# State-space stage: steps handled in two halves, row stores dealt out over the steps, the skip term as a product on TensorE

## The reference, cut to what matters

```
xn    = rms_norm(resid) * norm_w
skip  = xn @ skip_w.T ;  x = silu(conv4(xn @ in_w.T) + conv_b)
delta = softplus(x @ wd1.T @ wd2.T + wd2_b) ;  B = x @ wB.T ;  C = x @ wC.T
h[e,n] = exp(delta[e] * A[e,n]) * h[e,n] + delta[e] * x[e] * B[n]      # over time
y[e]   = sum_n h[e,n] * C[n] + W_D[e] * x[e]
out    = resid + (y * silu(skip)) @ out_w.T
```

## Time and profile before

| | us |
|---|---|
| median of 3 runs | 2874.22 (2873.86 to 2876.11) |
| profiled execution, its own time | 2880.12 |
| its span, first to last instruction | 2878.4 |
| first piece of `mamba` on TensorE | at 813.5 |
| first scan (L1114) | at 969.9 |
| last step's product (L1122) | starts at 2044.3 |
| experts' first TensorE work | at 2074.6 |

### The profile page before, as it was taken

The page is one execution under the profiler, slowest core; times in us unless marked ns, Lnnn a source line. Parts: engine busy times, 40 slices in busy tenths (PEclk is TensorE's granted clock), DMA queues, the critical chain, the costliest instruction groups (busy, mean ns, idle before and its releaser), DMA issues. The chain is left out here.

```text
span 2878.4 us, 33375 instructions
## 1 busy us (share of the span) xinstructions
PE 2290.2 (80%) x10578; PEld 1579.3 (55%) x10578; DVE 1978.3 (69%) x2641; ACT 1324.5 (46%) x2201; POOL 1167.5 (41%) x579
## 2 busy tenths in 40 slices
PE   1789999988713578888888887978599999999960
PEld 0677777776500223333323332323299999999960
DVE  6564555565400478888898988899588888888844
ACT  1333222233112555555556555643277666676630
POOL 1120221222055969787887878795100000000026
PEclk7899999999855689998989899978799999999985
DMA  6011100111042001111010111010265555555545
GB/s 229 15 37 36 36 5 31 36 36 36 26 165 83 21 31 37 37 37 37 37 52 29 46 37 37 30 51 22 73 235 212 212 215 220 222 222 221 220 128 187
DMA packets 109900, 264.86 MB, mean 92 GB/s; under 512 B 15796, under 2 KB 88516, under 8 KB 95124
## 3 DMA queue, kind: packets, MB, share of 16 engines
q1 hardware_dynamic: 103700, 247.41, 23.9%
q0 software_dynamic: 6144, 16.79, 1.8%
HBM read 213.89 MB, written 50.27 MB: 92 GB/s over the span
## 5 line engine op out<-in xcount | busy, mean ns | idle before, releaser
L946 POOL TENSOR_TENSOR m_work<-m_ux,m_bb 128x2048 f32<-128x2048 f32 x128 | 578.4, 4525 | 197.1 <-DVE m_hh L1114 196.4
L1187 PE MATMUL m_y<-m_work,m_ident 128*128 128x512 f32 x1024 | 553.8, 691 | 0.8 <-DVE m_work L1122 0.8
L1058 ACT ACTIVATE m_da<-m_dl,m_A 128x512 f32<-128x512 f32 x512 | 347.9, 687 | 304.5 <-DVE m_hh L1114 304.3
L1114 DVE TENSOR_TENSOR_SCAN m_hh<-m_da,m_work 128x512 f32<-128x512 f32 x256 | 295.7, 1207 | 230.4 <-POOL m_work L946 157.7
L1187 PEld LDWEIGHTS m_y<-m_work,m_ident 128*128 128x128 f32 x1024 | 213.9, 220 | 346.6 <-issue 345.0
L1602 PE MATMUL e_h<-e_xTh,e_w1h 128*128 128x256 f32 x1248 | 356.0, 285 | 16.8 <-DVE e_xTl L1538 16.8
L1671 POOL DMA_INDIRECT c_ya<-scratch_yg,c_dst x64 | 66.1, 1033 | 732.8 <-DMA c_wts<-scratch_wts 713.6
L1602 PE MATMUL e_h<-e_xTh,e_w1l 128*128 128x256 f32 x1248 | 351.7, 282 | 0.0
L1602 PE MATMUL e_h<-e_xTl,e_w1h 128*128 128x256 f32 x1248 | 351.6, 282 | 0.0
L1114 DVE TENSOR_TENSOR_SCAN m_hh<-m_da,m_carry,m_work 128x512 f32<-128x512 f32 x256 | 310.4, 1267 | 58.4 <-ACT m_da L1058 45.3
L1122 DVE TENSOR_TENSOR m_work<-m_hh,m_cb 128x2048 f32<-128x2048 f32 x128 | 292.8, 2288 | 11.4 <-issue 0.4
(11 more groups left out here) (238 smaller groups left out, 4664.0 us busy)
## 6 DMA issues: line engine op xcount, KB each, us to landing
e_w<-in_w SPq DMA_DIRECT2D x39, 2048.0 KB, 7.5
e_w<-in_w SPq DMA_DIRECT2D x39, 1024.0 KB, 9.5
m_bb<-scratch_bT SPq DMA_DIRECT2D x32, 1024.0 KB, 4.6
e_xg<-scratch_xg SPq DMA_DIRECT2D x39, 256.0 KB, 9.6
scratch_yg<-e_yo SPq DMA_DIRECT2D x39, 256.0 KB, 9.7
scratch_xg<-x1p SPq DMA_DIRECT2D x19, 512.0 KB, 7.8
e_b<-in_b SPq DMA_DIRECT2D x39, 128.0 KB, 8.7
xt<-in_x SPq DMA_DIRECT2D x9, 512.0 KB, 5.7
```

The source lines that it names most:

```text
L946: pool.tensor_tensor(bx[:, g % NB], ux[q % 2][:], slot.to_broadcast([P, KE, T]), ALU.mult).then_inc(s_bx, 1)
L1058: act.activation(da[e % 2][:], dl[q % 2][:, e], ACT.Exp, scale=A[:, at:at + 1]).then_inc(s_exp, 1)
L1114: dve.tensor_tensor_scan(hh[:, e], da[e % 2][:], bx[:, g % NB, e], 0.0 if q % 2 == 0 else carry[:, n, e:e + 1], ALU.mult, ALU.add).then_in ...
L1187: last = mm(y[:, e], ident[:], hc[:, g % 2, e], start=(n == 0), stop=(n == NST - 1))
```

## The change

1. **Half steps.** VectorE handles blocks 0 and 1 (two scans, then their product with C's row), then blocks 2 and 3. The product has half the length and there are two of them. The waits on `s_hc` and `s_carry` count halves. ScalarE's `extra` is cut in two: a half behind `decay(g, 3)` and a half behind `decay(g + 1, 1)`; the copy for `carry` is cut in two as well.
2. **A new table of slots.** One piece per step, issued between the sums of the first half and those of the second (`MID`). The input projections move to n = 10 and 12 to 14 of the chunk before the last one, O1 from n = 5 to n = 9, and ScalarE's copies with them (O1's is at n = 10, second half).
3. **Row stores dealt out.** GpSimd issues one of the 64 indirect stores every second step; SyncE loads the rows a block of 128 at a time into a buffer of their own.
4. **Skip term.** Four 128x128 diagonal matrices of `W_D` are made once by ScalarE. At n = 0, TensorE starts `y` with `diag * x`; L1099 is gone.
5. **C's broadcast.** `spread(g + 1)` is issued when the second half's product is done, ahead of the second half's sums (behind the first half's and the piece); at n = 0 it is ahead of all four sums, behind the piece, the wait for `finish` and the skip products.
6. **Softplus.** GpSimd's `(z + 1) - 1` (L919) becomes two ScalarE instructions; one of GpSimd's sums moves from n = 11 to n = 12. ScalarE's relu is written to `dl` directly. `conv` of block 0 moves to n = 15 of the chunk before, the others to n = 0 to 2.
7. The output rows are stored in two halves.

```diff
-    ahead = {0: ["IN2"], 1: ["IN3"], 2: ["SK0", "SK1"], 3: ["SK2", "SK3"], 4: ["O0"], 5: ["O1"], 6: ["BD"], 7: ["DT0", "DT1"],
-             8: ["DT2", "DT3"], 14: ["IN0"], 15: ["IN1"]}
+    TOP, MID = 0, 1
+    ahead = {(n, MID): [g] for n, g in enumerate(("SK0", "SK1", "SK2", "SK3", "O0", "BD", "DT0", "DT1", "DT3", "O1",
+                                                  "IN0"))}
+    ahead |= {(12 + e, MID): [f"IN{e + 1}"] for e in range(KE - 1)}
+    TAKEN = [(11, 1), (13, 0), (14, 0), (15, 0)]
+    ahead[8, TOP] = ["DT2"]
...
         @block.gpsimd
...
+                if n == NST - 1 and q + 2 < NCH:
+                    conv(q + 2, 0)
...
+                if n < KE - 1:
+                    conv(p, n + 1)
+                if n == 11:
+                    pool.wait_ge(s_wm, 2 * p + 2)
+                    pool.tensor_tensor(w, ez, w, ALU.subtract).then_inc(s_c, 1)
+                if n == 12:
+                    pool.wait_ge(s_c, p + 1)
                     pool.wait_ge(s_ln, p + 1)
                     pool.tensor_tensor(lw, lw, w, ALU.add).then_inc(s_lw, 1)
                     pool.wait_ge(s_lw, p + 1)
+                    pool.tensor_tensor(dl[p % 2][:], lw, dl[p % 2][:], ALU.add).then_inc(s_dl, 1)
...
             for g in range(STEPS):
                 if g + 2 < STEPS:
                     inputs(g + 2)
+                if g % 2 == 0:
+                    spread_rows(g // 2)
                 extra(g // NST, g % NST)
...
         @block.scalar
...
+            for e in range(KE):
+                act.activation(diag[:, e], ident[:], ACT.Copy, scale=column("W_D", e)).then_inc(s_diag, 1)
...
+            def extra(q, n, half):
+                p, p2 = q + 1, q + 2
+                if 0 <= p2 < NCH:
+                    if (n, half) in TAKEN:
+                        take_in(p2, TAKEN.index((n, half)))
+                    if n >= 14:
+                        taps(p2, n - 14, half)
                 if 0 <= p < NCH:
                     if n < 2:
+                        taps(p, n + 2, half)
+                    if 1 <= n < 5 and half == 0:
+                        take_skip(p, n - 1)
+                    if n == 4 and half == 1:
                         silu(p)
+                    if n == 6 and half == 0:
                         take_rows(p)
                     if n in (7, 8):
+                        take_step(p, 2 * (n - 7) + half)
                     if n == 9:
+                        wait_drained(act, f"DT{2 * half + 1}", p)
+                        both = ez[:, HALF * half:HALF * (half + 1)]
+                        act.activation(both, both, ACT.Exp, scale=-1.0).then_inc(s_ez, 1)
                     if n == 10:
+                        act.wait_ge(s_ez, 2 * p + 2)
+                        if half == 1:
+                            act.wait_ge(s_wm, 2 * p + 1)
+                        act.activation(w, ez if half == 0 else w, ACT.Identity, bias=1.0 - 2.0 * half).then_inc(s_wm, 1)
+                    if n == 11 and half == 0:
                         act.activation(lw, ez, ACT.Ln, bias=1.0).then_inc(s_ln, 1)
+                if q > 0 and (n, half) in ((5, 0), (10, 1)):
+                    take_out(q - 1, half)
...
                 decay(g, 2)
+                keep(g, 0)
                 decay(g, 3)
+                extra(q, n, 0)
                 if g + 1 < STEPS:
                     decay(g + 1, 0)
+                keep(g, 1)
                 if g + 1 < STEPS:
                     decay(g + 1, 1)
+                extra(q, n, 1)
...
         @block.vector
...
-                for e in range(KE):
-                    dve.scalar_tensor_tensor(out=y[:, e], in0=xs[p % 2][:, e], scalar=column("W_D", e), in1=y[:, e],
-                                             op0=ALU.mult, op1=ALU.add).then_inc(s_yf, 1)
-                dve.wait_ge(s_yf, (p + 1) * KE)
...
+                for j in range(2):
+                    cols = slice(HALF * j, HALF * (j + 1))
...
+                    for e in range(cols.start, cols.stop):
+                        dve.wait_ge(s_exp, g * KE + e + 1)
+                        dve.tensor_tensor_scan(hh[:, e], da[e % 2][:], bx[:, g % NB, e],
+                                               0.0 if q % 2 == 0 else carry[:, n, e:e + 1], ALU.mult, ALU.add).then_inc(s_scan, 1)
+                    if n == 0 and j == 1 and q > 0:
+                        finish(q - 1)
+                    dve.wait_ge(s_cb, g + 1)
...
+                    dve.tensor_tensor(hc[:, g % 2, cols], hh[:, cols],
+                                      cb[:].rearrange("p (o t) -> p o t", o=1).to_broadcast([P, HALF, T]), ALU.mult).then_inc(s_hc, 1)
...
         @block.tensor
...
+                pieces(q, n, TOP)
+                if n == 0:
+                    pieces(q, n, MID)
+                    if q > 0:
+                        pe.wait_ge(s_y1, q)
+                    pe.wait_ge(s_silu, 2 * q + 1)
+                    for e in range(KE):
+                        mm(y[:, e], diag[:, e], xs[q % 2][:, e], start=True, stop=False)
+                    pe.wait_ge(s_hc, 2 * g + 2)
                     spread(g + 1)
+                for j in range(2):
+                    pe.wait_ge(s_hc, 2 * g + j + 1)
+                    if j == 1 and n > 0 and g + 1 < STEPS:
+                        spread(g + 1)
+                    for e in (HALF * j, HALF * j + 1):
+                        last = mm(y[:, e], ident[:], hc[:, g % 2, e], start=False, stop=(n == NST - 1))
+                    if j == 0 and n > 0:
+                        pieces(q, n, MID)
```

More of the change, by code:

```diff
@@ L798, in mamba @@
         ux = [sb(f"ux{h}", [P, KE, T]) for h in range(2)]
-        brow = [sb(f"brow{h}", [2 * NST, T]) for h in range(2)]
-        dr = sb("dr", [DR, T])
+        drb = sb("drb", [DR + 2 * NST, T])
+        dr = drb[0:DR]
+        brow = [drb[DR:DR + 2 * NST], sb("brow1", [2 * NST, T])[:]]
+        diag = sb("diag", [P, KE, P])
         bb = sb("bb", [P, 2, NG, T])
@@ L803, in mamba @@
         bx, hc = work[:, 0:NB], work[:, NB:NB + 2]
[L804 removed]
+        rows = sb("rows", [P, 2, D])
         hh = sb("hh", [P, KE, T])
[L806 removed]
+        mo = sb("mo", [P, 2, D])
         dst = sb("dst", [P, NPICK], I32)
@@ L962, in _ @@
                     inputs(g + 2)
+                if g % 2 == 0:
+                    spread_rows(g // 2)
                 extra(g // NST, g % NST)
+            for i in range(2):
+                pool.wait_ge(picks_out[i], 16 * NPICK // 2)
         @block.scalar
@@ L972, in take_in, with taps @@
                 act.activation(region(p, e), rb[:], ACT.Copy).then_inc(drained, 1)
-            def taps(p, e):
+            def taps(p, e, half):
                 wait_drained(act, f"IN{e}", p)
@@ L980, in taps @@
                 at = (p % 2) * T
-                for k in range(PAD):
+                for k in (0, 1) if half == 0 else (2,):
                     act.activation(pk[:, e % 2, k], xpad[:, e, at + k:at + k + T], ACT.Copy, scale=conv_w(e, k)).then_inc(s_pk, 1)
-                act.activation(pk[:, e % 2, PAD], region(p, e), ACT.Identity, scale=conv_w(e, PAD),
-                               bias=column("conv_b", e)).then_inc(s_pk, 1)
+                if half == 1:
+                    act.activation(pk[:, e % 2, PAD], region(p, e), ACT.Identity, scale=conv_w(e, PAD),
+                                   bias=column("conv_b", e)).then_inc(s_pk, 1)
             def take_skip(p, e):
@@ L1012, in take_out @@
                 wait_filled(act, f"O{j}", p)
-                if p >= 1:
-                    act.wait_ge(mo_out, 16 * p)
-                act.activation(mo[:, 2 * j:2 * j + 2], rb[:].rearrange("p (s d) -> p s d", s=2), ACT.Copy).then_inc(drained, 1)
-            def extra(q, n):
-                p = q + 1
-                if n >= 14 and 0 <= q + 2 < NCH:
-                    take_in(q + 2, n - 14)
-                    if n == 15:
-                        taps(q + 2, 0)
+                if 2 * p + j >= 1:
+                    act.wait_ge(mo_out, 16 * (2 * p + j))
@@ L1058, in decay, with keep @@
                 act.activation(da[e % 2][:], dl[q % 2][:, e], ACT.Exp, scale=A[:, at:at + 1]).then_inc(s_exp, 1)
+            def keep(g, j):
+                q, n = g // NST, g % NST
+                if q % 2 == 0:
+                    act.wait_ge(s_scan, g * KE + HALF * (j + 1))
+                    if q >= 2:
+                        act.wait_ge(s_scan, ((q - 1) * NST + n + 1) * KE)
+                    cols = slice(HALF * j, HALF * (j + 1))
+                    act.activation(carry[:, n, cols], hh[:, cols, T - 1], ACT.Copy).then_inc(s_carry, 1)
             act.wait_ge(s_pad, 1)
-            extra(-2, 14)
-            extra(-2, 15)
-            for n in range(NST):
-                extra(-1, n)
+            for q, n in slots[:6 + NST]:
+                for half in range(2):
+                    extra(q, n, half)
             decay(0, 0)
@@ L1150, in piece @@
                     wait_drained(pe, "BD", p)
```

(24 more changed lines are left out.)

163 lines of the change are left out of this document (69 added, 94 removed).

## The result

The changed kernel takes 2749.4 us (median of 4 runs, 2746.4 to 2761.7), the kernel before 2874.0 (4 runs, 2873.7 to 2876.1). The ratio is 0.957, 95% interval [0.954, 0.960]: 124.6 us less. The run of 2761.7 had a mean granted clock of 0.88, the three others 0.92 to 0.93. The profiled execution took 2748.59 us and its span is 2746.8, 131.6 shorter than the span of before. The other 7 us are that before's profiled execution lay 6.1 over the median of these runs and this one 0.8 under its own.

A forecast was written before the change was run, and what follows sets the result against it. VectorE was taken to set the steps' pace, behind a chain at the head. -63.4 - 4.5 - 2 - 121 + 81 = -110, from 2880.1 to 2770, less 5.9: 2764 us; range 2708 to 2815, its own 2740 to 2790.

The forecast's parts named there:

- Head: Before the first scan: stores gone from ahead of the first convolution, L919 on ScalarE, one convolution moved ahead; -63.4 us.
- Tail: After the last product: the last four L1099 instructions go and only half of the sums is left; -4.5 us.
- VectorE's own work: VectorE in the steps: half products and paired scans cost +17 us, the L1099 groups removed save 19; net -2.
- The old waits: VectorE's waits in the steps for ScalarE's decay and GpSimd's inputs, plus small gaps for C's row: removed whole, -121 us.
- the new waits: VectorE's waits in the half steps, counted from zero over the eight chunks: 81 us in sum.
- IN0 behind O1: Input projection at n = 10 waits for the output piece's late copy, delaying C's row: 2.5 us a chunk.
- The boundary: Between chunks: skip products delay the broadcast (1.2 us), GpSimd's late convolutions delay decays (0.6 and 2.7): 4.5 us.
- The clock as a term of its own: TensorE's broadcast at the lower clock level after idling: 1.4 us a chunk, 12 us in chunks 1 to 5.
- Row stores: GpSimd's stores in the steps: 8 a chunk, 10.2 us, hidden except at chunk boundaries; bounds of one 0.97 and 3.0.
- B: Steps: most new waits don't come, 30 us instead of 81, giving 2713 us; chance 0.2.
- C: TensorE's queue: sums and piece ahead of C's broadcast at low clock cost 43 us more, giving 2804; chance 0.24.
- D: TensorE becomes the bound of the steps, with granted clock under 0.74; slower, for instance 2895 us; chance 0.04.

The follow-up runs named there:

- the second trace of the change: The changed kernel run again unchanged on the chip of the follow-up runs: 2752.4 us (5 runs), ratio 0.9579 to the kernel before.

## Why the forecast was right, and where its steps were off

The forecast was 2764 us (2708 to 2815), the result 2749.4, inside the likeliest case's own range (2740 to 2790). Between the two profiled executions the difference is larger: -110 forecast, -131.6 measured. It came from steps that were mis-sized; from the medians it is only 15, as before's profiled execution lay 6.1 us over its kernel's median and the new one 0.8 under.

**Head**, -63.4 forecast, -65.3 measured. The chain was read rightly: the table load is at 849.08 (850.7 forecast) and the first scan at 904.55 (906). The first convolution, at 826.35, came 1.8 us before its forecast, mostly because the stage's first loads had landed 1.4 us earlier (TensorE's first piece starts at 812.14, before at 813.50).

**Tail**, -4.5 forecast, -8.1 measured. The four instructions and half of the sums went as said. What was missed is the output piece: 3.69 us after an idle of 2.48 here, where the tail of before had 6.37 after 5.24. With the skip term back on VectorE it was 5.50 after 5.24. The last 0.8 us are an earlier start of the experts' TensorE work.

**VectorE's own work**, -2 forecast, -15 measured (the steps' -58.1 less the waits' 121 to 78); this is the term that was most wrong. The timeline of chunk 0, with nothing waiting:

```profile
928.38 2.33 DVE L1154 TENSOR_TENSOR_SCAN m_hh<-m_da,m_work 128x512 f32<-128x512 f32 x2
930.80 1.22 DVE L1162 TENSOR_TENSOR m_work<-m_hh,m_cb 128x1024 f32<-128x1024 f32 x1
931.94 2.33 DVE L1154 TENSOR_TENSOR_SCAN m_hh<-m_da,m_work 128x512 f32<-128x512 f32 x2
934.36 1.22 DVE L1162 TENSOR_TENSOR m_work<-m_hh,m_cb 128x1024 f32<-128x1024 f32 x1
935.50 2.33 DVE L1154 TENSOR_TENSOR_SCAN m_hh<-m_da,m_work 128x512 f32<-128x512 f32 x2
```

A step takes 7.12 us (928.38 to 935.50; 7.16 forecast), against 7.03 before, and one of an odd chunk 7.36 (7.40 forecast) against 7.28. The product is 1.221, but the next scan starts 1.14 after it, an overlap of 0.08; with the gap of 0.09 in front of the product the two nearly cancel, as forecast. The extra cost of halves is thus 0.08 to 0.09 a step, 11 us, not 17: several terms were each rounded up by a few hundredths. The skip term's 19 us went: a boundary took 2.7 us less, seven times. The other 6 or 7 us can be accounted for by an estimate: 56 of the old waits for ScalarE split a run of four scans, which then took 2 x 2.34 instead of 4.57 us, 0.11 each and 6 us in all. The change's 23 waits all stand in front of a pair. So the waits that went had cost more than their idle time.

From the rule of the Trainium skill ("VectorE: DVE Perf Modes", Rules for kernel authors), that the pipe drains after each instruction, the prediction had estimated 0.25 us a step. The trace disagrees with that: the fixed part is there (2 x 1.221 against 2.288, so 0.15 a step), the gap isn't, and 0.08 to 0.09 remain.

**The old waits** went and **the new waits** came to 78 us, 81 forecast. The sum is better than its items, which is partly luck: the waits at n = 11 came out longer than forecast and those at the boundaries, the clock's share counted in, shorter. VectorE's waits in chunk 1:

```profile
1036.30 2.46 DVE L1154 TENSOR_TENSOR_SCAN m_hh<-m_da,m_carry,m_work 128x512 f32<-128x512 f32 x2 [1.37 <-ACT m_da L1094]
...
1041.45 1.22 DVE L1162 TENSOR_TENSOR m_work<-m_hh,m_cb 128x1024 f32<-128x1024 f32 x1 [2.69 <-PE m_cb L1214]
...
1049.57 1.22 DVE L1162 TENSOR_TENSOR m_work<-m_hh,m_cb 128x1024 f32<-128x1024 f32 x1 [0.84 <-PE m_cb L1214]
...
1072.09 1.22 DVE L1162 TENSOR_TENSOR m_work<-m_hh,m_cb 128x1024 f32<-128x1024 f32 x1 [0.53 <-PE m_cb L1214]
...
1075.73 2.46 DVE L1154 TENSOR_TENSOR_SCAN m_hh<-m_da,m_carry,m_work 128x512 f32<-128x512 f32 x2 [2.42 <-ACT m_da L1094]
...
1111.84 1.22 DVE L1162 TENSOR_TENSOR m_work<-m_hh,m_cb 128x1024 f32<-128x1024 f32 x1 [0.53 <-PE m_cb L1214]
...
1123.03 1.22 DVE L1162 TENSOR_TENSOR m_work<-m_hh,m_cb 128x1024 f32<-128x1024 f32 x1 [3.93 <-PE m_cb L1214]
```

- The silus: 2.42 (3.0 forecast), and the same in every chunk but the first (3.10).
- O1: 0.53, in even chunks 0.77 (0.6). O0 costs the same, just ahead of the silus. I had it covered by their wait, which it isn't: that wait stands behind it.
- IN0 behind O1, at n = 11: 3.93, in chunks 1 to 5 between 2.70 and 4.35 (2.5 forecast). The place and the cause were right; the size wasn't, as I had IN0 at the upper level. It comes after an idle of 3.09 us and takes 3.42. Chunk 4 is the check: there it took 1.98 after the same idle, and the wait was the 2.70:

```profile
1118.52 3.42 PE L1184 MATMUL m_rb<-m_xr,m_w_si 128*128 128x512 f32 x4 [3.09 <-ACT m_mo L1052]
...
1505.14 1.98 PE L1184 MATMUL m_rb<-m_xr,m_w_si 128*128 128x512 f32 x4 [3.06 <-ACT m_mo L1052]
```

- The boundary: 1.37 + 2.69 + 0.84 = 4.9 in chunk 1, 2.8 to 3.4 in chunks 2 to 6 and 3.9 in chunk 7 (4.5). The 2.69 is again the clock, the skip products at 6.50 us after an idle of 3.42. In chunk 3 they took 3.70 after the same idle, and the product behind them waited 0.34. The granted clock was 0.80 from 1028 to 1045 and 1.00 from 1290 to 1302:

```profile
1033.86 6.50 PE L1229 MATMUL m_y<-m_xs,m_diag 128*128 128x512 f32 x8 [3.42 <-DVE m_spare L1140]
...
1293.64 3.70 PE L1229 MATMUL m_y<-m_xs,m_diag 128*128 128x512 f32 x8 [3.42 <-DVE m_spare L1140]
```

- The clock as a term of its own, 1.4 a chunk, is thus found inside the last two.

**Row stores.** 1.015 us each with some 0.16 of issue, in the forecast's range of 0.97 to 3.0 and near its lower end; in the steps they cost 9 to 14 us, as the stores put back at the head show, where I had them hidden outside the boundary.

**The reasons.** This is where the prediction read the old kernel wrongly, though its sum held. It took ScalarE's lateness as too much side work in one place. The first of its two examples, the wait of 4.41 us, would not be there without something else, ScalarE's own wait for a piece of TensorE just before its copy and taps:

```profile
1261.74 0.60 ACT L972 ACTIVATE m_xpad<-m_rb 128x512 f32<-128x512 f32 x1 [4.65 <-PE m_rb L1143]
```

Over the steps ScalarE was idle 157.5 us for such pieces in 76 places; in the change it is 16.5 us in 16. With whole products, its side work still cut in two, it is 141 us; with one slot and half products 23. So it is mainly the half products that took the old waits away, as they let TensorE start its piece earlier. The half slots of 3.3 us have another use: the kernel with one slot lost some 80 us with hardly any late decay. What joins the three engines is the queue of TensorE: copy out of the bank, piece, broadcast, product. The half products start that chain half a step earlier and the half slots free its bank. Undone one by one the parts cost 81 (halves), 51 (stores) and 16 us (skip term), from the ratios 0.9862, 0.9757 and 0.9636 less 0.9579, times 2872. That is 148, more than the 121 of the whole: they lean on each other.

**The rivals.** B expected under 35 us of new waits, C over 60 for C's row alone; 78 and 40.9 speak against both. D's clock of 0.74 is far from 0.95. The longest idles of TensorE in the steps became shorter: 6.9 to 7.7 us at the seven boundaries before, 1.5 to 5.1 now. The skip products have a part in the clock: from 905 to 1940 it was 0.93 without them and 0.92 with the broadcast ahead of them. What the even table adds wasn't run by itself.

**Sums that don't come out.** By its own terms the upper bound of the halves is 0.16 + 0.11 + 0.18 = 0.45 a step, 58 us and not 44. D's example, 147 us a chunk, gives some 2907 us and not 2895. D's 0.04 and the unseen loss's 0.02 make 0.06 for slower, not 0.04. The forecast rests on none of them.

## What to carry to other kernels

Trace an indirect store or any batch that merely shares a queue with the first operation of a chain, and deal it out: 64 stores at the head were worth 41 us net in the old order and some 50 in the new. Where several pieces of work share a bank and one queue, the time of the copy out sets the time of everything queued behind the next piece, so count slack along that chain and not on the engine with the most work. Before moving a product past a wait in TensorE's queue, look at what would then fill its idle time.

## What the runs showed of the hardware

Behind an idle, TensorE's next matmuls often took nearly twice their time: the broadcast 2.04 instead of 1.12 us (after 4.39 and 5.75 us), four matmuls of IN0 3.42 instead of 1.98 (after 3.09), eight skip products 6.50 (after 3.42) against 3.70 for eight sums. The length of the idle alone doesn't decide it. In the same trace the skip products of chunks 3 and 5 took 3.70 us after the same 3.42, and IN0 of chunk 4 took 1.98 after 3.06. In the kernel before a broadcast took 2.04 after only 2.31 us of idle (at 1354.72) and another 1.09 after 3.72 (at 1482.77). The places also change from one execution to the next: in the second trace of the change the skip products of chunk 1 took 3.70 (after 1.74) and those of chunk 2 5.40 (after 3.17), where the first has 6.50 (after 3.42) and 3.70 (after 1.48). I had looked for this only after the 7.67 us of the earlier trace rows. Work placed in such a gap raised the granted clock (0.93 without the skip products, 0.95 with them). How much of their 16 to 20 us comes from that isn't shown, as the four instructions that they replace are 22 us by themselves.

VectorE's consecutive instructions overlap by 0.08 to 0.09 us also where a scan follows a product, not only between scans; a product that needs the scan in front of it starts 0.09 us after its end.
